# Splitting the low-weight pass over the last 64 features of an up-projection into two 64-row matmul tiles

## The reference, cut to what matters

```python
def _L0_ffn_ref(x, router_w, w1, w2):          # x is the layer norm of h
    ...                                        # comb: top-8 weights of 16 experts
    for e in range(NUM_EXPERTS):               # 8 experts of width 128, 8 of width 256
        h = jax.nn.gelu(xt @ w1[:, off:off + wd])
        out = out + comb[:, e:e + 1] * (h @ w2[off:off + wd, :])
```

## Time and profile before

| what | value |
|---|---|
| time, median of 3 runs | 900.02 us (899.71 to 900.04) |
| span of the profiled execution, first to last instruction | 894.0 us |
| what lies around the span | 6.0 us against the median |
| PE busy, matmuls | 834.3 us (93%), 6048 matmuls |
| DVE busy | 574.6 us (64%) |
| ACT busy | 495.9 us (55%) |
| mean granted TensorE clock | 0.969 of full speed |

### The profile page before, as it was taken

How to read it: one execution, slowest core, us unless ns; L and a number is a source line. 1 busy time by engine, 2 the same in 40 slices (tenths; PEclk the granted TensorE clock), 3 DMA queues, 4 the chain that set the end, 5 groups by cost and what they waited for, 6 DMA issues and landing times.

```text
span 894.0 us, 18035 instructions
## 1 busy us (share of the span) xinstructions
PE 834.3 (93%) x6048; PEld 764.7 (86%) x6048; DVE 574.6 (64%) x1574; ACT 495.9 (55%) x1102; POOL 88.6 (10%) x162
## 2 busy tenths in 40 slices
PE   5879999999999995779999999999999999999996
PEld 2757878797787874579999999999999999999996
DVE  6657788888888774685565555655655655655554
ACT  1467787887787785434444444444444444444443
POOL 3111131220203021160000000000000000000000
PEclk9789999999999997779999999999999999999999
DMA  8300010101101027422532232232322322322320
GB/s 237 118 19 18 1 57 2 55 2 57 50 7 55 2 75 271 155 76 64 172 104 73 64 95 75 63 90 80 75 75 81 88 63 78 103 71 63 94 65 20
DMA packets 34421, 67.30 MB, mean 75 GB/s; under 512 B 3632, under 2 KB 14160, under 8 KB 34256
## 3 DMA queue, kind: packets, MB, share of 16 engines
q1 hardware_dynamic: 34384, 66.84, 25.3%
HBM read 55.41 MB, written 11.42 MB: 75 GB/s over the span
## 4 chain that ended last, share of the span: by engine, by line
PE 73%; issue 14%; DVE 6%; POOL 2%; ACT 2%; POOLq 2%; DVEq 0%; PEldq 0%; ACTq 0%; PEld 0%
PE ps L1085 67%; PE ps L1224 3%; DVE sc L841 1%; ACT xn L472 1%; PE ps L1124 1%; DVE pr L864 1%; DVE x L795 1%; POOLq L379 1%; POOL w_lo L402 1%; DVE out_r L1049 1%; PE ps L1441 1%; PE ps L1442 0%; PE ps L1303 0%; DVE den L856 0%; DVE w_lo L795 0%
## 5 line engine op out<-in xcount | busy, mean ns | idle before, releaser
L1031 DVE TENSOR_TENSOR act<-act,gate 128x548 f32<-128x548 f32 x192 | 141.0, 738 | 202.8 <-ACT act L681 202.8
L681 ACT ACTIVATE act<-ps 128x548 f32<-128x548 f32 x192 | 120.5, 628 | 247.9 <-PE ps L1085 245.6
L1085 PE MATMUL ps<-x_all,w_hi 128*128 (+1 forms) x1152 | 252.9, 292 | 0.9 <-ACT act L681 0.9
L1085 PE MATMUL ps<-x_all,w_lo 128*128 (+1 forms) x768 | 216.4, 290 | 0.0
L1085 PEld LDWEIGHTS ps<-x_all,w_hi 128*128 128x128 f32 x1152 | 195.0, 190 | 1.2 <-PEq L236 1.0
L1085 PEld LDWEIGHTS ps<-x_all,w_lo 128*128 128x128 f32 x768 | 146.1, 190 | 0.0
L795 DVE TENSOR_TENSOR act_lo<-act,act_hi 128x548 fp32r<-128x548 f32 x192 | 141.6, 738 | 1.3
L459 ACT ACTIVATE act_hi<-act 128x548 fp32r<-128x548 f32 x192 | 125.7, 655 | 19.4 <-DVE act L1031 19.4
L1085 PE MATMUL ps<-act_hi,w_hi 128*128 128x274 f32 x384 | 112.7, 294 | 6.7 <-DVE act_lo L795 4.1
L1085 PE MATMUL ps<-act_lo,w_hi 128*128 128x274 f32 x384 | 111.6, 291 | 0.0
L1085 PE MATMUL ps<-act_hi,w_lo 128*128 128x274 f32 x384 | 111.6, 291 | 0.0
(11 more groups left out here) (189 smaller groups left out, 1309.3 us busy)
## 6 DMA issues: line engine op xcount, KB each, us to landing
gate<-comb_dram SPq DMA_DIRECT2D x128, 274.0 KB, 3.3
x_all<-x_dram SPq DMA_DIRECT2D x8, 822.0 KB, 5.0
x_dram<-x SPq DMA_DIRECT2D x7, 822.0 KB, 3.4
w_raw<-w SPq DMA_DIRECT2D x8, 384.0 KB, 3.6
out<-h SPq DMA_DIRECT2D x8, 384.0 KB
w_others<-w SPq DMA_DIRECT2D x1, 2304.0 KB, 10.4
h<-txt SPq DMA_DIRECT2D x3, 672.0 KB
decay_rows<-drow SPq DMA_DIRECT2D x1, 1014.0 KB, 8.6
```

Source lines behind the costliest of these rows:

```text
L681: a.activation(act[k % 3][:, :, :], ps[:, 2 * (k % 2):2 * (k % 2) + 2, 0:HALF], ACT.Gelu_apprx_tanh).then_inc(gelu_done, 1)
L1031: dve.tensor_tensor(act[k % 3][:, :, :], act[k % 3][:, :, :], gate[e % 4][:, :, :], ALU.mult).then_inc(gated, 1)
L1085: return pe.matmul(dst, w, x, start=start, stop=stop)
```

## The change

The fifth pass of each half (w1_lo with chunk 2) is taken out of the series. After both halves have done their other four passes, two matmuls of 64 rows follow, which multiply w1_lo by the high part alone: for the first half on partitions 0 to 63, for the second half on partitions 64 to 127. They write different PSUM banks. So that the second half finds its high part on partitions 64 to 127, `x2_rest` puts the low rest of the tokens from 274 on onto partitions 0 to 63; the third subtraction of `x2_rest` becomes two for that. The product of w1_lo with the low part of the last 64 features is no longer computed. The TensorE loop over sequences 1 to 6 becomes straight code.

```diff
                     if i == 0:
                         sub(dst[:, 1, 512:L], ps[:, bank, X2_AT:X2_AT + LAST], dst[:, 0, 512:L])
-                        last = sub(dst[HD:P, 2, 512:L], ps[HD:P, bank, X2_AT + 64:X2_AT + 64 + LAST], dst[HD:P, 2, 512:L])
+                        last = sub(dst[0:HD, 2, 512:L], ps[0:HD, bank, X2_AT + 64:X2_AT + 64 + LAST], dst[0:HD, 2, 512:L])
...
-                        last = sub(dst[HD:P, 2, 0:512], ps[HD:P, 7, :], dst[HD:P, 2, 0:512])
+                        sub(dst[HD:P, 2, 0:HALF], ps[HD:P, 7, 0:HALF], dst[HD:P, 2, 0:HALF])
+                        last = sub(dst[0:HD, 2, HALF:512], ps[0:HD, 7, HALF:512], dst[0:HD, 2, HALF:512])
...
+                bank = 2 * (k % 2)
+
+                def x(p0, p1, c, n):
+                    return x2_all[p0:p1, b, c, n * HALF:(n + 1) * HALF]
                 for n in parts:
-                    def x(c):
-                        return x2_all[:, bass.ds(b, 1), c, n * HALF:(n + 1) * HALF].rearrange("p a n -> p (a n)")
-                    last = series(ps[:, 2 * (k % 2) + n, 0:HALF],
-                                  [(w1_hi[:, 0, w], x(0)), (w1_lo[:, 0, w], x(0)), (w1_hi[:, 0, w], x(1)),
-                                   (w1_hi[:, 1, w], x(2)), (w1_lo[:, 1, w], x(2))])
+                    for i, (wt, c) in enumerate(((w1_hi[:, 0, w], 0), (w1_lo[:, 0, w], 0), (w1_hi[:, 0, w], 1), (w1_hi[:, 1, w], 2))):
+                        mm(ps[:, bank + n, 0:HALF], wt, x(0, P, c, n), i == 0, False)
                 if 1 in parts:
-                    last.then_inc(up_done, 1)
+                    mm(ps[:, bank, 0:HALF], w1_lo[0:HD, 1, w], x(0, HD, 2, 0), False, True)
+                    mm(ps[:, bank + 1, 0:HALF], w1_lo[HD:P, 1, w], x(HD, P, 2, 1), False, True).then_inc(up_done, 1)
...
-            with pe.Fori(1, B - 1) as b:
+            for b in range(1, B - 1):
                 ffn(b, True)
```

## The result

The changed kernel takes 947.41 us (median of 4 runs, 945.88 to 947.73), the kernel before 899.87 us in the runs beside it: a ratio of 1.0532 [1.0510, 1.0555], 47.5 us more. The forecast was 951.6 us.

A forecast was written before the change was run, and what follows sets the result against it. PE's back-to-back matmuls, 0.127 us each, were taken to bound the second phase. Ups 49.4 + sequence ends 0.9 + first phase 1.3 = 51.6 us more: span 945.6, time 951.6 us, range 942 to 976.

The forecast's parts named there:

- The pair runs as one step: In each up, the two 64-row matmuls run side by side in one step, saving 0.127 us.
- The rival in series: Rival: the two 64-row matmuls of an up take two steps, no saving, 974.6 us; chance 0.11.
- A change of height: Each switch between 128-row and 64-row matmuls, two per up, costs PE 0.195 us in emptying and exposed weight load.
- Loads not exposed: Rival: after the emptying the next weights are already in place, a switch costs 0.09 us, 912.2 us; chance 0.05.
- Faster: Rival: no emptying between up and down, the pair simply saves a step, 878.3 us at zero switch cost; chance 0.03.
- The clock: Rival: more pauses cost PE its full clock, 274 us on top, about 1,230 us; chance 0.03.
- The loop: TensorE's loop over sequences turned into straight code was taken to cost 0.
- The sequence ends: At seven sequence ends, removing a pass before the transposes only lengthens PE's wait for the accumulators: +0.9 us.
- the term of the first phase: Splitting the third subtraction of x2_rest adds 0.16 us on the chain, over eight sequences +1.3 us.
- only moves from one partition half to the other, with the same size: First phase: the 36-token subtraction changes partition half at unchanged size, with no cost or gain counted.
- the first four ups as hidden: The four ups before the first down cost nothing, covered by PE's 3.3 us wait; uncovered they would cost 1.1 us.
- the 6.0 us around the span: Added to the forecast span of 945.6 us to give a time of 951.6 us, from span 894.0 and median 900.0.

The follow-up runs named there:

- one_group: The changed kernel with both 64-row matmuls on partitions 0 to 63, unable to run side by side, nothing mirrored or split: 972.02 us.
- own_switch: The changed kernel with each 64-row matmul right behind its own half's four full passes, four height changes per up and no pair: 1041.3 us.
- shared2: The kernel shared with ACT's and DVE's queues in the same order of twos (gelu, gelu, round, round; weigh, weigh, rest, rest): 912.6 us.
- half_rows2: Against the kernel before, all feed-forward matmuls as side-by-side pairs of 64-row tiles, ACT and DVE queues tile by tile: 877.96 us, ratio 0.9783.
- straight: The kernel before with only the TensorE loop over sequences 1 to 6 written out as straight code: 900.03 us, ratio 1.0010.
- shared: The changed kernel with ups taken two at a time, both pairs of 64-row matmuls behind one change of height, then two downs: 986.32 us.
- no_low: The changed kernel without the two 64-row matmuls, so w1_lo times the last 64 features is missing from the output: 867.4 us, ratio 0.9624.
- move_only: The kernel before with only the first phase's 36-token subtraction moved from partitions 64 to 127 onto 0 to 63: 895.13 us.
- split_only: The kernel before with only the first phase's third subtraction split into 274 and 238 tokens, both on partitions 64 to 127: 899.14 us.
- full_height: The changed kernel with the last two matmuls of each up at the full 128 rows again, all else kept: 898.79 us, ratio 1.0010.

## Why the prediction was right

The sign, the size and the mechanism were right, by the steps as they stood; one small term was wrong:

- **The pair runs as one step.** 0.003 us between the two, forecast within 0.02. The rival in series is excluded: where the pair is forced into series (one_group), the kernel takes 972.02 us.
- **A change of height costs 0.19 us, emptying and exposed load** (forecast 0.195). The trace gives (0.262 + 0.127) / 2 = 0.194. The times give it four times over, once the side effects (-0.19 us a sequence in the first phase, taken for all eight, and +0.9 us at the sequence ends) are taken out where the kernel has them. This table is worked out from the medians, with 0.127 us a step:

| kernel | us over before | equation for c, the price of one change | c |
|---|---|---|---|
| after | 47.5 + 1.5 - 0.9 = 48.1 | 188 (2c - 0.127) | 0.191 |
| one_group | 72.7 - 0.9 = 71.8 | 188 x 2c | 0.191 |
| own_switch | 142.1 + 1.5 = 143.6 | 188 x 4c | 0.191 |
| shared2 | 14.0 + 1.5 - 0.9 = 14.6 | 202c - 188 x 0.127 | 0.191 |

  The intervals of the ratios are worth 0.005 to 0.016 us in c, so that the agreement in the third digit is luck. But from 202 to 752 changes give one price within that: the cost is that of the change of height itself and not of this pair or this place. "Loads not exposed" would have been 0.09. "Faster" would have needed c under 0.063.
- **The Trainium skill** says in "TensorEngine Tiling (Array Packing)", section "Key Properties", that a change of tiling mode drains TensorE. The trace of the changed kernel agrees: the first 64-row load starts 0.21 us behind the last 128-row matmul's start, 0.09 us more than a step. The same page of the Trainium skill, section "Theoretical Speedup", has up to 2x where one dimension is at most 64. half_rows2 agrees, where no change of height stands between the tiles: two 64-row matmuls run in each step of 0.127 us.
- **The clock** stayed at its upper level in the second phase from 400 us on, 1.00 in the window from 400 to 942 us. Ahead of that, from 380 to 390 us, it is 0.50, and 0.76 in the kernel before.
- **The loop** costs nothing that can be told: straight is within its interval of before, which reaches from -0.7 to +2.4 us.
- **The sequence ends** cost the 0.9 us of the forecast.

**Where the sum was off.** The forecast put the span at 945.6 us; the profiled one is 944.1. Span against span, 51.6 us were forecast and 50.1 came.

The step that failed is the term of the first phase, +1.3 us. The split itself was sized rightly on the way to the logits (0.16, measured 0.17), but "only moves from one partition half to the other, with the same size" was priced at nothing, and the move saves 0.23 us a sequence; and by the spacing the split costs less than by the way to the logits, since `gst` behind it starts sooner. Instead of 0.16 us longer a sequence got 0.19 us shorter. The two chains show it from 140 us on: from the block of 65 matmuls to the last piece that both have alike go 328.38 - 140.22 = 188.16 us before and 327.78 - 140.55 = 187.23 after, 0.93 us less. Eight sequences would make -1.5 us; ahead of 140 us the two chains have no common piece to compare.

Some of that was lost again where the phases meet: the first long run of matmuls starts at 390.36 us, 0.67 us later than the 389.69 of before. The forecast had taken the first four ups as hidden, but in the chain the gelu behind the first `up` starts at 378.60 us instead of 377.96. PE's windows there (375 to 378.6 us, and 376 to 378 before) have a granted clock of 0.50, and 1.00 before; how much of the delay is the clock and how much the changes of height no run separates. From there to the end go 553.7 us, 49.4 more than before, where 49.4 + 0.9 were forecast.

The other miss is the 6.0 us around the span. Every run with a span on record has 1.7 to 1.9 us there, and the median of 900.02 came from runs with a longer span than the profiled one. The 4.2 us by which the forecast time lies above the measured 947.41 are this term alone; that the median runs have the forecast's span of 945.6 us is luck.

**What was wrong in the experiments' expectations.** For shared and no_low I counted PE's steps alone. PE was the bound only as long as the others' queues delivered in its order; move or remove PE's work, and the order of gelu and rounding on ACT decides. In the changed kernel it did not: PE only became slower, and its waits list none for `act_lo`.

## What to carry to other kernels

Where TensorE sets the end and its matmuls follow each other without gaps, a smaller tile between full ones must save more than two changes of height, here 0.39 us or three steps of 274 columns; the pair of half-height passes here saved one step. Gather more than three such pairs behind one change (by these prices; two still lost 14 us), or give the whole stage one height: then half-height passes side by side are worth half a step each, and this kernel came to 877.96 us. Before reordering the bound engine's work, read the order of the queues that feed it; a producer's queue in the old order can cost more than the change saves.

## What the runs showed of the hardware that I had not expected

- A DVE subtraction starts before the one ahead of it has ended where both start on the same partition, 0.07 to 0.08 us before that end; where one starts on partition 0 and the other on 64, it starts 0.01 to 0.03 us after the end. So it is in the traces of before, move_only, split_only and after, seven times each (but for two starts that came 0.16 us after the end). It is the change that counts and not the half: the two halves of split_only, both on 64 to 127, overlap too. The 36-column subtraction on 64 to 127 stood between two that start on partition 0; moved, it takes away two such changes, 0.20 us, it lasts 179 ns instead of 199, and the 512-column one behind it, which did not move, 677 ns instead of 692. From the groups by shape of the kernel with the move alone (busy us, mean ns):

```profile
L795 DVE TENSOR_TENSOR x<-ps,x 128x512 fp32r<-128x512 f32 x7 | 4.7, 677 | 0.0
...
L795 DVE TENSOR_TENSOR x<-ps,x 64x36 fp32r<-64x36 f32 x7 | 1.3, 179 | 0.0
```

  Whether it is the operands in PSUM, those in SBUF or the result that must start alike, no run here tells.
- Runs of one kernel differ: full_height's ten are 894.77 to 895.73 (three), 898.68 to 898.80 (three) and 903.59 to 903.93 us (four). Between the phases, at 350 to 360 us, the changed kernel's granted clock is at the lower level (1.2 GHz), where PE's work has gaps and the DMA engines are 0.73 busy (columns as in the earlier trace rows):

```profile
350.00:360.00 10.00, 7.35 (x34) 6.80 (x35) 4.83 (x15) 5.49 (x12) 2.41 (x4) 0.50 0.73 257
```

  How long that lasts differs from profile to profile, and full_height's mean granted clocks go with its times: 0.972 in the three fastest runs, 0.963 to 0.967 in the next three, 0.961 in the four slowest. That the one makes the other was not tested.
